# Output projection of a masked attention layer: plain float32 on four 128x32 column tiles in place of split halves

## What is computed

```
q, k, v = x @ Wq + bq, x @ Wk + bk, x @ Wv + bv        # heads of 32
scores  = q @ k.T * scale;  scores = -inf where adj == 0
out     = softmax(scores) @ v                          # [128, 64, 512]
y       = out @ Wo + bo                                # the output projection
result  = layernorm(x + y)
```

## Time and profile before

| | |
|---|---|
| median of 3 runs | 838.52 us (836.79 to 838.89) |
| profiled execution, its time | 838.44 us |
| profiled execution, span of the core | 836.6 us |
| TensorE busy | 817.4 us, 98% |
| VectorE, GpSimd, ScalarE busy | 547.6, 516.9, 230.5 us |
| mean granted TensorE clock | 0.991 of full speed |

### The profile page before, as it was taken

One profiled execution on the slowest core, in us unless ns is written; L12 is line 12 of the kernel. 1 busy time (PEld: TensorE's weight loads), 2 busy tenths in 40 slices (PEclk: granted clock), 3 DMA queues, 4 the chain that ended last, 5 costly groups with the idle time before them and its releaser, 6 DMA issues.

```text
span 836.6 us, 25496 instructions
## 1 busy us (share of the span) xinstructions
PE 817.4 (98%) x11273; PEld 669.8 (80%) x11273; DVE 547.6 (65%) x694; ACT 230.5 (28%) x305; POOL 516.9 (62%) x401
## 2 busy tenths in 40 slices
PE   8999999999999999999999999999999999999984
PEld 6887888888888888888888888888888888888863
DVE  4657667766567766567666667666667665677785
ACT  6522233222233221233222233222332222322110
POOL 1275767656575665767656675665856657665366
PEclk9999999999999999999999999999999999999988
DMA  8223424243342433424253242433434343322433
GB/s 332 71 77 99 138 77 133 84 141 101 89 134 74 140 99 102 131 76 131 83 154 95 74 145 70 145 102 88 126 88 127 95 139 97 85 77 81 129 79 106
DMA packets 50173, 92.37 MB, mean 110 GB/s; under 512 B 11280, under 2 KB 13328, under 8 KB 47888
## 3 DMA queue, kind: packets, MB, share of 16 engines
q1 hardware_dynamic: 48720, 88.65, 36.1%
q10 hardware_dynamic: 1344, 2.10, 0.8%
HBM read 40.37 MB, written 16.78 MB: 68 GB/s over the span
## 4 chain that ended last, share of the span: by engine, by line
PE 89%; DVE 4%; POOL 2%; SPq 1%; DMA 1%; issue 1%; ACT 1%; ACTq 0%; POOLq 0%; DVEq 0%
PE ring L265 21%; PE ring L266 20%; PE ring L267 19%; PE ring L343 6%; PE ring L342 6%; PE ring L346 6%; PE psum_s L316 6%; PE ring L331 5%; SPq L201 1%; DVE top L582 1%; POOL row L177 0%; POOL qt L177 0%; ACTq L486 0%; POOL soft L167 0%; DMA qt<-in_wq 0%
## 5 line engine op out<-in xcount | busy, mean ns | idle before, releaser
L717 POOL TENSOR_TENSOR soft<-soft,top 128x1024 f32<-128x1024 f32 x62 | 125.5, 2024 | 80.2 <-DVE top L582 80.2
L167 POOL TENSOR_TENSOR soft<-soft,inverse 128x1024 f32<-128x1024 f32 x62 | 119.0, 1919 | 25.4 <-DVE inverse L589 22.7
L467 ACT ACTIVATE kt<-ring,bk 128x512 f32<-128x512 f32 x64 | 43.6, 681 | 279.4 <-PE ring L267 279.4
L694 POOL TENSOR_TENSOR x_lo<-x_raw,x_hi 128x512 fp32r<-128x512 f32 x56 | 71.9, 1285 | 60.9 <-ACT x_hi L452 60.9
L265 PE MATMUL ring<-wv_hi,x_hi 128*128 128x512 f32 x256 | 103.0, 403 | 1.7 <-ACT kt L467 1.4
L586 DVE TENSOR_REDUCE total<-soft 128x16 f32<-128x1024 f32 x62 | 75.6, 1220 | 42.4 <-ACT soft L472 42.4
L265 PE MATMUL ring<-x_hi,wk_hi 128*128 128x512 f32 x256 | 103.0, 402 | 0.0
L265 PE MATMUL ring<-x_hi,wq_hi 128*128 128x512 f32 x256 | 100.4, 392 | 1.1 <-DVE x_lo L623 1.1
L266 PE MATMUL ring<-x_lo,wq_hi 128*128 128x512 f32 x256 | 100.1, 391 | 0.0
L267 PE MATMUL ring<-x_hi,wq_lo 128*128 128x512 f32 x256 | 100.0, 391 | 0.0
L266 PE MATMUL ring<-wv_lo,x_hi 128*128 128x512 f32 x256 | 99.9, 390 | 0.0
(11 more groups left out here) (74 smaller groups left out, 1369.4 us busy)
## 6 DMA issues: line engine op xcount, KB each, us to landing
pt<-soft SPq DMA_DIRECT2D x488, 64.0 KB, 2.0
x_raw<-in_xt SPq DMA_DIRECT2D x15, 1024.0 KB, 7.0
row<-in_x SPq DMA_DIRECT2D x60, 256.0 KB, 2.9
out_rows<-row SPq DMA_DIRECT2D x60, 256.0 KB, 2.6
adj<-in_adj SPq DMA_DIRECT2D x16, 128.0 KB, 2.7
kt<-in_wk SPq DMA_DIRECT2D x4, 256.0 KB, 7.0
row<-in_wv SPq DMA_DIRECT2D x1, 1024.0 KB, 8.7
soft<-in_wo SPq DMA_DIRECT2D x1, 1024.0 KB, 10.5
```

Source lines behind the costliest of these rows:

```text
L167: ops.tensor_tensor(soft_of(c), soft_of(c), on_keys(inverse[:, c % 2, :]), ALU.mult).then_inc(done, 1)
L694: nc.gpsimd.tensor_tensor(x_lo[:, buf, :, rows], x_raw[:, :, rows], x_hi[:, buf, :, rows].bitcast(F32), ALU.subtract).then_inc(x_lo_done, 1)
L717: nc.gpsimd.tensor_tensor(soft_of(c), soft_of(c), on_keys(top[:, c % 2, :]), ALU.subtract).then_inc(centred, 1)
```

## The change

The output projection multiplies `ot` and `wo` as plain float32, with no halves. The 128x128 array is addressed as four column tiles of 128 rows by 32 columns: for each chunk there are four calls, each with 32 of the 128 rows of the output as its weights, and each with all 512 columns of `wo` moving. They write four groups of 32 partitions of one bank. `ot` is one copy by ScalarE, `split_ot` is gone, Wo is loaded into memory of its own and isn't split. The waits on `ot_lo_done` go, the first projection waits for the load of Wo instead of its halves. The warm-up matmuls take their zeros from `x_hi`.

```
-        w_hi = [sb(f"w{n}_hi", [P, KC, D], F32R) for n in "qkvo"]
-        w_lo = [sb(f"w{n}_lo", [P, KC, D], F32R) for n in "qkvo"]
+        w_hi = [sb(f"w{n}_hi", [P, KC, D], F32R) for n in "qkv"]
+        w_lo = [sb(f"w{n}_lo", [P, KC, D], F32R) for n in "qkv"]
+        wo = sb("wo", [P, KC, D])
-        ot_hi = sb("ot_hi", [P, 2, KC, P], F32R)
-        ot_lo = sb("ot_lo", [P, 2, KC, P], F32R)
+        ot = sb("ot", [P, 2, KC, P])
-            sp.dma_start(w_raw[3], w_dram[3]).then_inc(w_in[3], DMA)
+            sp.dma_start(wo[:, :, :], w_dram[3]).then_inc(w_in[3], DMA)
             def project_out(c):
-                pe.wait_ge(ot_hi_done, c // 2 + 1)
+                pe.wait_ge(ot_done, c // 2 + 1)
                 if c == 0:
-                    pe.wait_ge(w_hi_done, 4 * KC)
-                    pe.wait_ge(w_lo_done, 4 * KC)
+                    pe.wait_ge(w_in[3], DMA)
+                    pe.sem_inc(pe_went_on, 1)
                 for kc in range(KC):
-                    nc.tensor.matmul(y_bank(c), ot_hi[:, c % 2, kc, :], w_hi[3][:, kc, :], start=kc == 0, stop=False)
-                    nc.tensor.matmul(y_bank(c), ot_hi[:, c % 2, kc, :], w_lo[3][:, kc, :], start=False, stop=False)
-                pe.wait_ge(ot_lo_done, c // 2 + 1)
-                for kc in range(KC):
-                    last = nc.tensor.matmul(y_bank(c), ot_lo[:, c % 2, kc, :], w_hi[3][:, kc, :],
-                                            start=False, stop=kc == KC - 1)
+                    for n in range(HC):
+                        part = slice(n * SQ, (n + 1) * SQ)
+                        last = nc.tensor.matmul(y_bank(c)[part], ot[:, c % 2, kc, part], wo[:, kc, :],
+                                                start=kc == 0, stop=kc == KC - 1)
-                nc.tensor.matmul(ring[:, 0, :], w_hi[3][:, 0, 0:P], w_hi[3][:, 0, :], start=True, stop=True)
+                nc.tensor.matmul(ring[:, 0, :], x_hi[:, 1, 0, 0:P], x_hi[:, 1, 0, :], start=True, stop=True)
-                pe.wait_ge(ot_lo_done, p)
-            pe.wait_ge(ot_lo_done, FULL)
-                nc.scalar.copy(by_chunk(ot_hi), mixed_rows(p)).then_inc(ot_hi_done, 1)
+                nc.scalar.copy(by_chunk(ot), mixed_rows(p)).then_inc(ot_done, 1)
             read_k(2)
-            split_w(3, 0)
-            split_w(3, 1)
             read_k(3)
-            split_w(3, 2)
-            split_w(3, 3)
-            def split_ot(p):
-                dve.wait_ge(ot_hi_done, p + 1)
-                nc.vector.tensor_tensor(by_chunk(ot_lo), mixed_rows(p), by_chunk(ot_hi).bitcast(F32),
-                                        ALU.subtract).then_inc(ot_lo_done, 1)
-            nc.vector.memset(w_hi[3][:, 0, :].bitcast(F32), 0.0).then_inc(warm_done, 1)
+            nc.vector.memset(x_hi[:, 1, 0, :].bitcast(F32), 0.0).then_inc(warm_done, 1)
-            for kc in range(KC):
-                split_w(3, kc)
-            dve.wait_ge(w_lo_done, 4 * KC)
+            dve.wait_ge(w_lo_done, 3 * KC)
-                if p >= 1:
-                    split_ot(p - 1)
-            split_ot(FULL - 1)
-            split_ot(FULL)
-            split_ot(FULL + 1)
```

More of the change, by code:

```diff
@@ L105, in attention_kernel @@
         mixed = sem("mixed")
-        ot_hi_done, ot_lo_done = sem("ot_hi_done"), sem("ot_lo_done")
+        ot_done = sem("ot_done")
         row_biased, row_added, row_stats = sem("row_biased"), sem("row_added"), sem("row_stats")
@@ L110, in attention_kernel @@
         pe_went_on, dve_went_on, pool_went_on = sem("pe_went_on"), sem("dve_went_on"), sem("pool_went_on")
-        w_raw = [qt[:, 1], kt[:, 1], row[:, :, :],
-                 soft[:, :, :, :, :].rearrange("p a b h k -> p (a b h k)").rearrange("p (c n) -> p c n", n=D)]
+        w_raw = [qt[:, 1], kt[:, 1], row[:, :, :]]
         def s_banks(n, m):
```

## The result

The changed kernel takes 878.83 us (878.08 to 879.46, 4 runs) against 838.70 us (836.79 to 838.99, 4 runs): 1.0483 times as long, with a 95% interval of 1.0464 to 1.0502. Its profiled execution has a span of 876.2 us, 39.6 more than before.

What follows compares the result with a forecast made beforehand. TensorE, gapless from about 35 to 805 us, was taken as the bound. The sum: 838.4 + 48.0 (projection) + 4 (tile shape) - 0.5 (start) - 1.5 (end) = 888.4 us, range 877 to 960.

Steps and rivals of the forecast that it cites:

- TensorE's stream bounds the kernel: From about 35 to 805 us TensorE streams without a gap, so a nanosecond there is a nanosecond of the kernel.
- A record streams its columns twice, a call four times: In the projection, a plain float32 record holds its tile for two streams of 512 columns, 426.7 ns; two records a call.
- The four tiles overlap fully: In the projection, a chunk's four calls run together, so a chunk is two rounds of 440 ns, 0.880 us.
- The two rivals that made it slower: Projection's weight loads exposed: 936 us, chance 0.16; halves of a call in strict order: 1118 us, chance 0.05.
- The overhead of a record: In the projection, 13.5 ns over the columns of each plain record, making 440 ns; bounds 427 and 464 ns.
- The change of shape: One new change of tile shape a pair, between `project_v` and `project_out`: 0.13 us, times 30 about 4 us.
- The start: Without the splits of Wo, the 1.4 us wait for `kt` may shrink: -0.5 us (0 to -1.4).
- The end: Three `split_ot` leave VectorE, so GpSimd's last chain starts some 1.5 us sooner: -1.5 us (-2.5 to +2).
- the first term: The 60 tiles that write to `ring`, 240 chunks at 0.200 us more each: 48.0 us (41.5 to 59.3).
- Faster, with one stream a record: In the projection, a record holds its tile for 227 ns, a chunk costs 0.454 us, the kernel 786 us; chance 0.10.

Runs made afterwards that it cites:

- experiment 2: The changed kernel with only the first of four column tiles, three quarters of the projection's output rows left out: 878.14 us, 1.0478 of before.
- experiment 1: The changed kernel with one plain float32 matmul of 128x128 weights a chunk in place of four on column tiles: 874.65 us, 1.0435 of before.
- Experiment 3: The changed kernel with the loops swapped, all four chunks on one column tile, then the next tile: 1157.83 us, 1.3820 of before.
- Experiment 5: Kernel before, plain whole array and plain column tiles, each with 256 of 512 columns moving in the projection: 794.8, 795.1 and 797.2 us.
- experiment 4: The changed kernel with the calls of two chunks in a row on one column tile, then the next tile: 880.32 us, 1.0514 of before.

## Why the prediction was right, and where it was off

The forecast was 888.4 us in a range of 877 to 960; the measured 878.83 lies near its lower end, and the direction was right. The sum added 50.0 us; the span grew by 39.6. Of the 10.4 us between them 6.0 lie in the 28 pairs (48.5 expected, 42.5 found), 3.2 at the end and 1.2 at the start. All three errors went the same way and brought the time to within 2 us of the bound of 877: the mechanism was right, but that the range held owes something to luck. By its steps:

**TensorE's stream bounds the kernel.** Right. All of TensorE's waits come to 5.5 us, and none lies between 35 and 800 us, where it is busy without a gap. A pair grew by 1.52 us, which is what the longer projection on TensorE accounts for, and VectorE's lost work moved nothing there.

**A record streams its columns twice, a call four times.** Right in time, by the distance between bursts (0.429 us at 512 columns) and by the 0.216 us at 256.

**The four tiles overlap fully.** Right; 16 bursts of four, and experiment 2. That the split gains nothing over one 128x128 call was right too (experiment 1). The two rivals that made it slower fell with this: no load came into the open, and the halves of a call don't hold back the next tile. Experiment 3 shows where that second one would have been true in part: with eight records in a row on one tile.

**The overhead of a record.** Mis-sized, and about half of the error. I took 13.5 ns from the float32r stream because it had the same number of columns; it measured 2.5. The lower bound that I had set, nothing, was the nearer. So was the fastest stretch of the same kind of record: the first rounds of `mix` take 60 ns for 53.3 ns of columns, 6.7 over the earlier trace rows. A chunk is 0.858 and not 0.880 us: 0.022 x 240 = 5.3 us. Experiment 5 shows what was wrong with the choice: the overhead goes with the kind of the record, not with its columns. The rule of the Trainium skill for back-to-back matmuls at the full clock is a fixed cost of about 2.5 ns a matmul over its columns (TensorE: Matmul & The Clock Gate, "Wait — 56ns, not 53.3ns?"). The plain records of these traces agree with it if it is taken once a record and not once for each of its two streams (429.2 over 426.7); the float32r records at 13.3 don't.

**The change of shape.** I took 0.13 us a pair. Right: the kernel without the new change is 0.13 us a pair faster (experiment 1), and 0.09 of it shows between `project_v` and the projection. With the chunk it makes 0.178 x 8 + 0.13 = 1.55 us a pair. The 28 pairs show 1.52, mainly because `score` and `mix` together take 0.06 us a pair less than before, which I had not counted.

**The start.** I took 0.5 us off and named 1.4 as the most; the wait of 1.4 us for `kt` vanished whole. Up to 75 us the kernels are level although one projection is 1.5 us longer. Another 0.3 us stood there at the first `score` (29.88 in place of 30.17). Ahead of it TensorE's matmuls started 0.43 us apart until 9.86 us before and until 7.04 us after, so the clock had come to its full level sooner, which the change doesn't account for.

**The end.** Mis-sized by 3 us. I forecast 1.5 us off, and wrote that TensorE's wait for the transfer would swallow the 1.6 us by which the projection of T-6 and T-5 gets longer. But I had also counted those 1.6 us among the 60 tiles of the first term, so the sum held them though the text said that they would not show. The rest is in ScalarE's issue of four transfers for T-3, which took 4.14 us in the profile before and here:

```profile
844.45 2.71 ACTq L481 DMA_DIRECT2D pt<-soft  x4
```

That is 1.4 us which no engine's work explains. It stands in one issue: the one at 804.02 takes 1.79 us in place of 0.6, and SyncE's beside it, at 803.76, 2.05. What goes together with it is a packet of 16 KB on the queue q8, which the profile calls `instruction`. In the kernel before one falls into 803.6 to 805.9, in the changed kernel none into 844.44 to 847.2. The queues in these stretches (packets, MB, share), before and after:

```profile
q1 hardware_dynamic: 93, 0.13, 23.2%
q10 hardware_dynamic: 91, 0.13, 21.8%
q8 instruction: 1, 0.02, 4.6%
```

```profile
q1 hardware_dynamic: 132, 0.19, 29.1%
q10 hardware_dynamic: 98, 0.14, 19.5%
```

This holds over the whole kernel before: 36 of the 512 issues of `pt` take over 1.05 us, and a packet of q8 starts within 0.6 us of the start of each of the 36; of the other 476 issues 38 have one so near. In experiments 1 and 2 the packet falls into the issue of T-4, which then takes 3.5 and 3.7 us, while that of T-3 takes 2.7. In all, q8 moved 1.46 MB before and 1.62 MB after, about 65 bytes for each matmul and weight load of TensorE in both (an estimate from the counts of the page). So it most likely brings TensorE's instructions, and a different number of them shifts where the packets fall. No run moved a packet and nothing else: that it holds the issue up is argued and not shown. The four transfers of T-3 take ScalarE 2.7 us in all seven kernels with 512 columns whose T-6 and T-5 are plain, and 3.3 to 4.1 us in the four kernels that keep the halves there. The length of that projection is not what decides: with 256 columns plain it is shorter than before, and the issue takes 2.8 us.

The two subtractions account for 1.9 us: `split_ot(FULL)` 1.2, and 0.7 for the one ahead of the sums of T-4. VectorE's multiplication of T-3 took 0.2 us longer. GpSimd's chain, which starts at 857.13 and closes the kernel as forecast, answers to the earlier trace rows:

```profile
857.13 0.19 POOL L701 TENSOR_TENSOR shifted<-moments,eps 128x1 f32<-128x1 f32 x1 [4.04 <-DVE moments L598]
```

From the `score` of T-4 to it there are 31.84 us, and 34.83 before: the 3.0 us are all gained ahead of it.

**Faster, with one stream a record.** It fell, by the 0.429 us a record. The durations at the low clock, which I had held against it, pointed the right way.

## What to carry to other kernels

Count the streams first: a product in split halves is three streams, a plain float32 call is four, and cutting the array into column tiles changes neither, since four tiles at once take as long as one. Where TensorE is the bound, plain float32 loses here. Where TensorE waits anyway and the engine that makes the halves does not, it might pay, but of four trials at the end of this kernel one stood clear of no change, by 0.3%; after a wait its four streams can run at the lower clock. Order calls so that neighbours use different tiles of the array; a run of two calls on one tile was free here, a run of four made the kernel take a third more. The overhead of an instruction went with its kind and not with its size: look for a row of the same kind first, at its densest.

## What was not expected of the hardware

A float32r matmul costs 13.3 ns over its columns at 256 and at 512 columns, a plain float32 record 2.5 ns. With three float32r matmuls a chunk that is 40 ns of 680.

TensorE works on past a busy column tile while no more than four of that tile's records are unfinished: with eight in a row (experiment 3) the next tile started exactly with the fifth, with four in a row (experiment 4) the pair took 7.08 us against 7.00.

An issue of a transfer of `pt` takes 0.5 to 0.9 us as a rule and up to 2.05 us where a packet of 16 KB of the queue q8 starts within 0.6 us of it: all 36 long issues of the kernel before, all 33 of the changed one. The cause is argued above and not shown.

A tile shape of 128x32 left the clock alone here: with one column tile of four at work, a quarter of the array, the granted clock was 1.00 through the whole loop, as with all four. The window of that kernel, with the clock after the five engines:

```profile
35.00:800.00 765.00, 765.00 (x9788) 513.43 (x9789) 443.53 (x569) 203.95 (x258) 468.12 (x355) 1.00 0.34 100
```
